# Latent attention with its own step orders: raw queries and keys copied out of PSUM, inputs normalised by ScalarE and GpSimd, a plain fp32 output product

## What is computed

```python
x = x + _L1_xattn_ref(ctx_768, _layernorm(x, axis=-1), mask_BxS2_bk0, ...)

def _L1_xattn_ref(x, latents, mask, ln_x_g, ln_x_b, ln_l_g, ln_l_b, qn_g, kn_g, Wq, Wkv, Wlkv, Wo, bo):
    xn = layernorm(x, ln_x_g, ln_x_b)                  # context: 128 rows of 96 columns
    ln = layernorm(latents, ln_l_g, ln_l_b)            # latents: 128 rows of 128 columns
    q = ln @ Wq.T
    kv = jnp.concatenate([xn @ Wkv.T, ln @ Wlkv.T], axis=1)
    k, v = (kv[..., :INNER], kv[..., INNER:])          # INNER = 128, 2 heads of 64
    qn = rmsnorm(q, qn_g) * SCALE
    kn = rmsnorm(k, kn_g)
    attn = jnp.einsum('bhid,bhjd->bhij', qn, kn)       # 128 queries, 256 keys
    attn = jnp.where(full_mask[:, None, None, :], attn, -jnp.finfo(attn.dtype).max)
    attn = jax.nn.softmax(attn, axis=-1)
    out = jnp.einsum('bhij,bhjd->bhid', attn, v)
    return out @ Wo.T + bo
```

## Time and profile before

| | us |
|---|---|
| median of 3 runs | 1567.12 (1560.07 to 1581.92) |
| the profiled execution: its own time | 1574.44 |
| its span, first to last instruction | 1572.7 |
| mean granted TensorE clock over the span | 0.877 |
| first instruction of the latent attention's DMA, to its last add into `x_all` | 976.8 to 1247.7 |
| PE, DVE, ACT, POOL busy in the stretch 976 to 1248 | 212.92, 169.11, 94.49, 101.87 of 272.00 |
| granted clock in that stretch | 0.79 |

### The profile page before, as it was taken

How to read it: one execution, slowest core, us unless ns; L and a number is a source line. 1 busy time by engine, 2 the same in 40 slices (tenths; PEclk the granted TensorE clock), 3 DMA queues, 4 the chain that set the end, 5 groups by cost and what they waited for, 6 DMA issues and landing times. The chain is left out here.

```text
span 1572.7 us, 33634 instructions
## 1 busy us (share of the span) xinstructions
PE 1264.9 (80%) x12396; PEld 913.7 (58%) x12396; DVE 936.4 (60%) x2150; ACT 627.5 (40%) x1120; POOL 774.4 (49%) x868
## 2 busy tenths in 40 slices
PE   2899997888888669996999997578888744199991
PEld 1577775555555546654677765467777643066660
DVE  3688875799999546654556554576666443133333
ACT  2354543345454135543545444233333321055550
POOL 3778774355664024435556552443433157445552
PEclk9999998799999759996999999696887755599996
DMA  9900000000000000000000000000000001344435
GB/s 349 370 14 9 2 3 13 13 25 14 14 7 2 1 1 1 1 0 1 2 2 3 2 2 7 11 6 10 5 5 1 1 30 46 108 125 138 142 94 161
DMA packets 58912, 68.43 MB, mean 44 GB/s; under 512 B 13182, under 2 KB 41731, under 8 KB 58640
## 3 DMA queue, kind: packets, MB, share of 16 engines
q1 hardware_dynamic: 52944, 56.92, 11.5%
q0 software_dynamic: 4992, 8.48, 1.6%
q10 hardware_dynamic: 832, 1.07, 0.2%
HBM read 32.76 MB, written 33.42 MB: 42 GB/s over the span
## 5 line engine op out<-in xcount | busy, mean ns | idle before, releaser
L582 DVE TENSOR_REDUCE maxes<-bank 128x8 f32<-128x1024 f32 x192 | 234.5, 1221 | 59.0 <-PE bank L383 57.6
L512 ACT ACTIVATE self_probs<-bank 128x1024 f32<-128x1024 f32 x128 | 129.2, 1023 | 44.6 <-PE bank L416 44.1
L1751 POOL DMA_INDIRECT returned<-relu_y,relu_rows x92 | 90.5, 984 | 96.1 <-DVE relu_y L1680 74.3
L723 POOL TENSOR_TENSOR self_k_hi_m<-self_kq_hi,const 128x512 fp32r<-128x512 f32 x64 | 66.6, 1041 | 79.2 <-ACT self_kq_hi L540 79.2
L519 ACT ACTIVATE self_neg_max<-bank 128x512 fp32r<-128x512 f32 x64 | 38.2, 597 | 154.8 <-PE bank L430 154.8
L1411 PE MATMUL bank<-relu_hidden,relu_w_tile 128*128 128x512 f32 x184 | 93.8, 593 | 0.0
L1469 ACT ACTIVATE relu_hidden<-bank,cols 128x512 f32<-128x512 f32 x92 | 63.2, 687 | 76.4 <-PE bank L1404 56.5
L2292 POOL TENSOR_TENSOR latent_inverse<-latent_norms_kept,latent_power 128x6 f32<-128x6 f32 x32 | 42.5, 1329 | 95.0 <-DVE latent_norms_kept L2150 89.8
L1671 DVE CAST relu_s_hi<-bank 128x512 fp32r<-128x512 f32 x23 | 15.9, 692 | 115.1 <-PE bank L1390 60.1
L588 DVE TENSOR_SCALAR bank<-bank 128x1024 f32<-128x1024 f32 x64 | 78.2, 1224 | 3.8 <-PE bank L404 3.7
L592 DVE RECIPROCAL self_recip<-bank 128x128 f32<-128x128 f32 x64 | 61.2, 957 | 28.5 <-PE bank L443 26.3
(11 more groups left out here) (392 smaller groups left out, 3657.6 us busy)
## 6 DMA issues: line engine op xcount, KB each, us to landing
routed<-blank SPq DMA_DIRECT2D x1, 20540.0 KB, 63.7
relu_w_tile<-in_w_ffn SPq DMA_DIRECT2D x23, 512.0 KB, 3.6
relu_rows<-routed SPq DMA_DIRECT2D x23, 260.0 KB
relu_back<-returned SPq DMA_DIRECT2D x16, 256.0 KB, 5.1
x_all<-in_x SPq DMA_DIRECT2D x8, 256.0 KB, 8.0
x_before<-x_all SPq DMA_DIRECT2D x8, 256.0 KB, 2.9
out_x<-x_all SPq DMA_DIRECT2D x8, 256.0 KB, 4.1
self_ctx_in<-in_ctx SPq DMA_DIRECT2D x8, 192.0 KB, 2.6
```

Of the source, the lines that this page charges most:

```text
L512: act.activation(probs[n % 2][:, 2 * pair:2 * pair + 2, :, :].rearrange("p u j q -> p (u j q)"), T[:, 2 * pair * GT:(2 * pair + 2) * GT], ...
L582: dve.tensor_reduce(out.rearrange("p j u -> p u j"), S.rearrange("p (u j k) -> p u j k", u=2, j=U), AX.X, ALU.max, negate=True).then_inc(m ...
L723: pool.tensor_tensor(out[n % 2][:, :, :], src[(n // GB) % 2][:, batch_cols(n)].bitcast(F32).unsqueeze(1).broadcast_to([P, U, P]), slots.un ...
L1751: pool.indirect_dma_start(returned[:, :], bass.IndirectOffsetOnAxis(ap=slots[t % NX][:, b, P:P + 1].bitcast(I32), axis=0), y[t % NY][:, b, ...
```

## The change

1. `copy_kq`: ACT copies raw queries and keys out of `PL` and `PC` into a new SBUF pair `kq`. `square` reads `kq` and is one instruction, `normalise` reads `kq` and is one instruction. The projection waits for `kq_done` and `v_done` of the batch before, not for `unit_done`.
2. The inputs' normalisation goes to ACT (`normalise_inputs`, with a shift made on POOL by two more small operations), the context's to POOL (`normalise_context`). The moments are two steps on DVE, `mx` for the inputs and `mc` for the context.
3. The output product is one plain fp32 matmul of `o_t` (two buffers, copied by ACT) with the unrounded `Wo`. `o_hi`, `o_lo` and the rounded parts of `Wo` go. The bias is added to a group of `x_all` on POOL (`add_bias`).
4. The slots' loop is gone: all steps are written out, in orders read from a new table `ORDERS["latent"]`. A step "P+5" is done in slot n for batch n + 5, "X^9" in slot n for the group that begins with batch n + 9, where there is one. `scores` waits only for `q_hi`; `key_scores` waits for `q_lo` and `k_lo`. A use of bank `M` waits for the semaphore of the use before it (`m_free`).
5. SP loads the next group's context when the one before is normalised (`c_normal`); `mc` of a group waits for that load.

```diff
+    "latent": {
+        "PE": "K+2 C^8 T+0 m+0 w-1 f+0 y-2 X^9 s+1 P+5 o-1",
+        "ACT": "v+3 sq+3 ax^8 e-1 ac^7 ln^10 oc-2 cp+4 kh+2",
+        "DVE": "mc^12 ss+3 M+0 mx^14 d+2 hc^7 hx^8 sp+0 u+3 kl+2 n-1 a-2",
+        "POOL": "cn^8 rs^11 ql+1 bo^8 iv+3 lx^7 lc^7",
     },
...
+        kq = [buf(f"kq{i}", [P, 3 * P]) for i in range(2)]
...
+            def project(n):
+                G = n // GB
+                pe.wait_ge(lo_done, max(remainders["lx", G], remainders["lc", G]))
+                if n > 0:
+                    pe.wait_ge(kq_done, 2 * n)
+                    pe.wait_ge(v_done, 2 * n)
...
-            def out_project(it, n):
-                pe.wait_ge(m_read, it * 24 + (turn['o', n] + 1))
-                pe.wait_ge(m_read, it * 24 + turn['y', n])
-                pe.matmul(M[:, 0:P], ident_r, bo_hi, start=True, stop=False)
-                pe.matmul(M[:, 0:P], ident_r, bo_lo, start=False, stop=False)
-                split_matmul(M[:, 0:P], (o_hi[:, :], o_lo[:, :]), (w_hi[:, 5 * P:6 * P], w_lo[:, 5 * P:6 * P]),
-                             start=False).then_inc(out_projected, 1)
...
+            def out_project(n):
+                pe.wait_ge(o_t_done, n + 1)
+                m_free(pe, "y", n)
+                pe.matmul(M[:, 0:P], o_t[n % 2][:, :], wo, start=True, stop=True).then_inc(out_projected, 1)
...
+            def copy_kq(n):
+                act.wait_ge(projected, n + 1)
+                if n - 1 > 0:
+                    act.wait_ge(unit_done, n - 1)
+                    act.wait_ge(squares_done, n - 1)
+                act.activation(kq[n % 2][:, 0:2 * P], PL[:, 0:2 * P], ACT.Copy).then_inc(kq_done, 1)
+                act.activation(kq[n % 2][:, 2 * P:3 * P], PC[:, 0:P], ACT.Copy).then_inc(kq_done, 1)
...
-                act.activation(squares[:, 0:2 * P], PL[:, 0:2 * P], ACT.Square).then_inc(squares_done, 1)
-                act.activation(squares[:, 2 * P:3 * P], PC[:, 0:P], ACT.Square).then_inc(squares_done, 1)
...
+                act.activation(squares[:, :], kq[n % 2][:, :], ACT.Square).then_inc(squares_done, 1)
...
+            def normalise_inputs(G):
+                act.wait_ge(rstd_done, G + 1)
...
+                    op = act.activation(xn[:, b, :], x_of(GB * G + b), ACT.Identity, scale=rstd[:, GB + b:GB + b + 1],
+                                        bias=shift_ln[:, b:b + 1])
...
+            def context_moments(G):
+                if G > 0:
+                    dve.wait_ge(c_mean_done, GB * G)
+                    dve.wait_ge(rstd_done, G)
+                    dve.wait_ge(c_normal, G)
+                dve.wait_ge(ctx_loaded, 16 * (G + 1))
...
-                for lo, hi, src in ((0, 2, PL[:, 0:2 * P]), (2, 3, PC[:, 0:P])):
-                    dve.tensor_tensor(unit[n % 2][:, lo:hi, :].rearrange("p a (h d) -> p (a h) d", d=DL),
...
+                dve.tensor_tensor(unit[n % 2][:, :, :].rearrange("p a (h d) -> p (a h) d", d=DL),
+                                  kq[n % 2][:, :].rearrange("p (h d) -> p h d", d=DL),
+                                  inverse[:, :].unsqueeze(2).broadcast_to([P, 3 * HL, DL]), ALU.mult)\
+                    .then_inc(unit_done, 1)
...
+            def normalise_context(G):
...
+                    op = pool.tensor_scalar(cn[:, b, :], ctx_in[:, b, :], mean_var[:, b, 0:1], rstd[:, b:b + 1],
+                                            ALU.subtract, ALU.mult)
...
+            def add_bias(G):
+                pool.wait_ge(x_normal, G + 1)
+                x = X[:, G * GT:(G + 1) * GT]
+                pool.tensor_tensor(x, x, bo.unsqueeze(1).broadcast_to([P, GB, P]), ALU.add).then_inc(biased, 1)
```

482 lines of the change are left out of this document (210 added, 272 removed).

## The result

| | before | after |
|---|---|---|
| median of four runs each, us | 1563.6 | 1514.7 |
| ratio with its 95% interval | 1 | 0.969 (0.964 to 0.974) |
| span of the profiled execution, us | 1572.7 | 1512.4 |
| the stage: first context load issued to last add into `x_all` ended, us | 270.9 | 214.5 |
| run-in: that load to the first reduction over `maxes`, us | 32.4 | 46.0 |

The change makes the kernel 3% faster, near the forecast of 1508 us. The stage accounts for 56.4 us of the 60.3 us by which the spans differ; the rest lies in stages that the change does not touch, which began this one 3.1 us earlier.

A forecast was written before the change was run, and what follows sets the result against it. PE was taken as nearest the bound, its waits costing twice through the low clock behind them. 31 x (7.30 - 5.35) = 60, less 1 for the ends, gave 59 us: 1515 profiled, 1508 on the median; range 1489 to 1548.

The forecast's parts named there:

- The spacing: Latent attention, time from batch to batch: from 7.30 to 5.35 us, low end 4.8, if the clock stays at 1.00.
- PEclk 1.00 from the fourth batch or so: Sign of success: TensorE's clock in the latent attention stays at full rate from about the fourth batch to the end.
- wrong if the clock falls once a group: Sign of failure: TensorE's clock in the latent attention drops once in every group of four batches.
- The rival that I gave 18%: Rival, 18%: a PE stop of 1.5 to 2 us per group keeps the clock falling; 6.4 us a batch, 1539 us.
- I count 0.4 us exposed, twice in four batches: New waits behind each group's moments on VectorE, for context and for inputs: 0.2 us a batch.
- The ends: The stage's run-in and run-out: +4 us before the first projection, -3 us at the end, net +1.
- The loads of the engines: Work a batch in the latent attention: DVE near 4.1 us, ACT and POOL near 4.0, all under PE's.
- The loop opened by the copy: Projection waits for copies, not squares, norms, power and `unit`; loop falls from five stages to two, was 8.5 us at low clock.
- The output product's order: Output product placed behind the weighting, so the 0.96 us wait for the add has weighting and shift in front of it.
- VectorE and GpSimd hinder each other: Rival, 12%: `unit` reads two SBUF tensors beside a busier GpSimd, losing 0.41 to 0.6 us a batch; 1525 us.
- The order gives it back: Rival, 10%: GpSimd's work bunched in every fourth batch makes `inverse` late; spacing 6.5 to 7.3 us, 1545 to 1567.
- slower: Rival, 5%: TensorE's array never leaves 1.2 GHz, 8.3 us a batch; +31 us, 1598 us.

The follow-up runs named there:

- e1: The changed kernel with two buffers for the context and for its means and variances; 1494.4 us, ratio 0.951.
- e7: The kernel of e1 with the output product ahead of the maxima's transpose and VectorE's add directly behind the maxima; 1515.3 us.
- e4: The kernel before with only the copy of raw queries and keys to SBUF by ScalarE added, all orders as before; 1555.3 us, ratio 0.989.
- e10: The kernel of e1 with the inputs' preparation one slot later on all engines, the projection left in place; 1496.8 us.
- e3: The changed kernel's operations in the orders of the kernel before; 1559.1 us, ratio 0.993.
- e5: The kernel of e1 with the projection four batches ahead instead of five; 1607.0 us, ratio 1.027.
- e9: The changed kernel with the context moments last in VectorE's slot and the reciprocal deviations last in GpSimd's; 1526.9 us, ratio 0.976.
- e11: The kernel of e1 with the context's normalisation at the end of VectorE's slot and the deviations at the end of GpSimd's; 1518.7 us.
- e6: The kernel of e5 with the projection also waiting for the unit vectors of the batch before; 1627.6 us, ratio 1.038.

## Why the prediction was right, point by point

**The total.** 1508 us was forecast, 1514.7 measured, a ratio of 0.963 against 0.969. Off the profiled time 59 us were forecast, and the two profiled spans differ by 60.3; but the medians differ by 48.9 only, since the profiled execution of the kernel before was one of its longer ones. So the forecast was some 10 us too good by the medians, and that it came so near is in part luck: several terms were wrong in opposite directions.

**The spacing, 5.35 us predicted, 5.20 measured.** The forecast was 5.15 us of PE work and 0.2 us of exposed moments at the full clock, for every batch. The steady part, in which groups are still prepared, is shown by three groups (twelve batches) of the kernel after and of e1:

```profile
1043.50:1115.10 71.60, 59.90 (x420) 55.89 (x420) 52.52 (x175) 42.51 (x138) 54.20 (x60) 0.93 0.04 10
```

```profile
1026.40:1089.50 63.10, 56.70 (x422) 51.98 (x422) 55.87 (x176) 42.35 (x138) 53.92 (x60) 1.00 0.04 11
```

At the full clock, in e1, PE is busy 4.7 us a batch: the work was put 0.4 us too high. I had taken 5.5 us from one batch of the earlier trace rows, in which stops are mixed with work, and had given back 0.25 for better cover. Part of that is the output product: it was taken as 0.4 us against 0.51 before, and counted in the same way, to the start of the next matmul, it is 0.24 in most batches. In the kernel after PE is busy 5.0 us a batch and idle 1.0 in a spacing of 6.0. So its mean clock of 0.93 costs about 0.3 us a batch, for which the forecast had nothing, and it stops for 1.0 us where 0.2 was forecast. In this part the spacing was 0.6 us over the forecast. Over the last twelve spacings it was 4.2 us, 1.1 under it, a phase that the forecast did not set apart. The mean of 5.20 is near 5.35 because the two errors nearly cancel: luck, not a right term. The low end of the range was also mis-added: 5.4 less five stops of 0.15 us is 4.65, not 4.8.

**"PEclk 1.00 from the fourth batch or so" and "wrong if the clock falls once a group".** By its own sign this step of the forecast failed: until 1122 us the clock falls in almost every group. The rival that I gave 18% had its mechanism right (moments late, PE stopped for about 3 us, clock low after it), its price too high: 1539 us, 31 over the forecast. e1 gives a price: 11 us in the spacing. The rival's rule from the Trainium skill (TensorE: Matmul & The Clock Gate, "A second HAM failure mode"), by which small frequent idles make the clock swing, is borne out in part. e1 is against it: it has stops of up to 0.9 us for `neg_max`, eight in 136 us, and its clock stays at 1.00. e7 is for it: PE stops for 0.47 us in every batch, and its clock falls for 3.4 us at 1050.3 and at 1094.7 us with no stop over 0.53 us in the 20 us ahead of either. In the kernel after it fell at each of the four stops of 2.8 to 3.2 us; stops of 1.60 us (kernel after, 1044 us) and 1.76 us (e1, 1018 us) went one without and one with a fall.

**"I count 0.4 us exposed, twice in four batches".** This is the step that failed. I priced four statistics and four aggregations (1.2 us; they last 0.74 to 0.96 and 0.38 us) and had named the wait for the load only in the run-in. In the steady part the context's moments wait for that same load, up to 3.6 us, and PE stops for 11.0 us in 25 batches at the maxima's transpose alone, 0.44 a batch. The order listing showed the moments at the head of VectorE's slot and the change listed that SP loads only after `c_normal`; what was missing was the question in which slot GpSimd gives `c_normal`: the same one.

**The ends, +1 predicted, +8.6 measured.** The run-out is 5.0 us shorter (-3 predicted), the run-in 13.6 us longer (+4 predicted). Run-in of the kernel after, in order of time:

```profile
981.34 2.72 POOL L2231 TENSOR_SCALAR latent_cn<-latent_ctx_in,latent_mean_var,latent_rstd 128x96 f32<-128x96 f32 x4
...
986.64 0.74 DVE L2112 BATCH_NORM_STATS2 latent_c_stats<-latent_ctx_in 128x6 f32<-128x96 f32 x4 [4.03 <-DMA latent_ctx_in<-in_ctx]
...
993.61 0.68 PE L1916 MATMUL bank<-latent_w_hi,latent_x_hi 128*128 128x384 f32 x1
...
998.88 0.74 DVE L2112 BATCH_NORM_STATS2 latent_c_stats<-latent_ctx_in 128x6 f32<-128x96 f32 x4 [6.38 <-DMA latent_ctx_in<-in_ctx]
```

I followed only the first projection; the third group's moments pay the load again (6.38 us), before the first maxima. With two buffers e1 has 9.0 of the 13.6 us back.

**The loads of the engines.** DVE 4.25 us a batch (4.1 predicted), POOL 4.2 (4.0), ACT 3.45 (4.0): near enough, and none of them the bound. VectorE waited 0.7 us in all for `inverse` (1024 to 1164 us), so that sign of failure did not come. The term for `cn` was mis-sized: 0.69 us alone on GpSimd (the minimum of its 32 is 0.678) where 0.4 was taken and 0.75 was the upper bound.

**The loop opened by the copy.** Right, and worth 16 to 18 us by itself (e4). The forecast gave it no price of its own, and so did not say that most of the gain needs the orders.

**The output product's order.** Right: 0.7 us a batch were expected to come back with the old place, 0.60 did (e7).

**"VectorE and GpSimd hinder each other" (12%).** They do, in the kernel after and in e1 about once a group. In e1, in order of time:

```profile
1060.49 1.28 POOL L2241 TENSOR_TENSOR latent_x_lo<-latent_xf,latent_x_hi 128x512 fp32r<-128x512 f32 x1
1060.56 1.62 DVE L2142 TENSOR_TENSOR latent_unit<-latent_kq,latent_inverse 128x384 f32<-128x384 f32 x1
...
1061.72 1.59 POOL L2241 TENSOR_TENSOR latent_c_lo<-latent_cf,latent_c_hi 96x512 fp32r<-96x512 f32 x1
```

`unit` lasts 0.54 us in most batches and 1.62 here, as if it did nothing until `x_lo` ended at 1061.77; `c_lo` then lasts 1.59 instead of 1.26 us. My 0.41 us from the earlier trace rows was too small for this pair. The whole-instruction exclusion that the Trainium skill states (SBUF — State Buffer, "SBUF: two separate sides") fits these rows, but not all. By the page whichever starts first keeps the other out to its end. In the kernel after:

```profile
1075.82 1.86 POOL L2240 TENSOR_TENSOR latent_c_lo<-latent_cf,latent_c_hi 96x512 fp32r<-96x512 f32 x1 [0.36 <-DVE latent_c_hi L2122]
1076.00 0.54 DVE L2141 TENSOR_TENSOR latent_unit<-latent_kq,latent_inverse 128x384 f32<-128x384 f32 x1
```

Here `unit` starts 0.18 us after `c_lo` and is not delayed; `c_lo` is the one that gets longer, by 0.6 us. In other places `unit` did wait with starts of 0.06 to 0.57 us behind `x_lo`, so what decides which of the two waits is not shown. It costs little because `unit` can never stand beside the norms' power: it needs its own batch's `inverse`, and the next one waits for `unit`. It meets `x_lo`, once a group, and now and then `q_lo` (1.09 us at 1138.07 us in the kernel after). e10 agrees, though it moves the inputs' steps as well: its `unit` is under 0.9 us from 1024 to 1118 us, and its spacing is that of e1. In the old orders it meets `q_lo` in half of the steady batches (e3). "`unit` over 0.9 us", one of my signs of failure, therefore occurred, and without harm that a run shows.

**The order gives it back (10%), and slower (5%).** Neither came. POOL's work in a group's heavy slot did not delay `inverse` to any length that PE saw. The runs e5, e9 and e11 show that orders of this kind can give all of it back, by one step in the wrong place.

**What stays open.** Of the 45 us of stage that the orders are worth, e7, measured from e1, names about 20 (the product's place), e10 shows that the inputs' lead could be a slot less, and the rest was not taken apart: the split of scores and key scores, the keys' transpose at the slot's start, and the projection's lead together with ScalarE's. What the closed loop would cost in the new orders is open too, since e6 was compared with a kernel that was held up elsewhere.

## What to carry to other kernels

When steps are put at hand-chosen leads, list for every wait both the slot in which the releaser's engine gives it and the slot in which the waiter asks, and add the DMA's time between them; a lead counts only between two engines, and a wait at the head of an in-order queue costs everything behind it. A buffer that is freed and wanted again in the same slot wants a twin; moving the steps about only moved the wait, from VectorE to GpSimd to ScalarE. And take an engine's work per batch from a stretch in which it hardly stops and has all of its work to do, not from one batch with stops in it, and forecast the phases of a stage apart.
